# Attention block with a gated expert layer: the last batch of the gating gets a lot of its own

## The chip, the core and the metric

The kernel runs on one core of one Trainium2 chip. The metric is the device time of one execution in microseconds; of the kernel before there are three runs. The core has five engines that run their own instruction streams and wait for each other through semaphores: TensorE (PE; PEld is its weight load), VectorE (DVE), ScalarE (ACT), GpSimd (POOL) and SyncE (SP), which here only issues DMAs. POOL issues the indirect DMAs (rows scattered or gathered by an index per partition).

## The reference

```python
x = x + attention(layernorm(x))           # x: [8, 512, 128], 16 heads of 8, causal, learned relative keys and values
h = layernorm(x)                          # 4096 tokens
scores = softmax(h @ gate_w.T)            # 8 experts
idx = top_k(scores + gate_bias, 2)
weights = scores[idx]
y = sum over e of gate_e * ((silu(h @ w1[e].T) * (h @ w3[e].T)) @ w2[e].T)      # gate_e: the weight, 0 if e is not chosen
z = (silu(h @ sw1.T) * (h @ sw3.T)) @ sw2.T                                      # two shared experts, 256 hidden
out = x + y + z
```

## The kernel before, in words

**Attention.** Two batch elements (32 heads) are worked together: four groups, each with four row tiles of 128 rows, in the order 2, 0, 1, 3 (`ROWS`). So there are 16 rows of work, called rows 0 to 15 here (in the code `e`); a row yields two tiles of 128 tokens. A row tile has eight quads of four heads; row tile 0 takes four heads in a unit (they are narrow), row tile 1 two, row tiles 2 and 3 one. The units, 352, are the slots `m` of one software pipeline. In a slot VectorE copies a turned probability tile (L1156) and takes the minima of the scores (L1171), ScalarE takes the exponentials (L1091), TensorE multiplies and turns (L920, L932, L949, L965), POOL masks the near probabilities (L867, L871, L875). SP moves the relative scores through HBM (`put_rel`, `get_near`), some slots ahead.

**Gating beside attention.** When a row is projected (`pj`), VectorE adds the residual and takes the moments (L1209, L1609, L1612), POOL normalises it (`normalise`, L1555 to L1570), TensorE turns it and takes the eight scores. Four rows, one group, are a batch. For a batch VectorE does a chain of 25 small steps (`chain_op`, L1677 to L1725), two to a slot: softmax, two maxima, weights, and, after a rank product of TensorE (`ranks`), the place of every token in its expert's region of the HBM tensor `slots`. `chain_slots` sets the slots. POOL then scatters the batch's 8 tiles twice, once for each chosen expert (`spread`, L1583, 16 indirect DMAs).

**Expert part.** Two lots: groups 0 to 2 (lot A) and group 3 (lot B). For a lot VectorE computes a map (`map_op`, 14 steps, L1744 to L1776): which expert and which region a block of 128 slots has. Two blocks are a pair; there are 28 pairs in lot A and 12 in lot B. The shared experts are cut into 24 items (for each of 8 chunks of 512 tokens two hidden products, L1851 and L1853, and one sum, L1862). `expert_steps` writes all 64 items into one list of steps that every engine follows: 8 shared items, the pairs of lot A with 12 shared items between them, the pairs of lot B with one, then 3 shared items. A pair takes five steps: turn (L1810), hidden products one step later (L1819), turn of the hidden state after three (L1827), product after four (L1834), and VectorE's weighing (`weigh`, L1927). POOL then scatters the pair's two blocks into the HBM tensor `parts` (`put_parts`, L1591, two indirect DMAs). SP loads a pair's two tiles six steps ahead (`load_pair`, L1457, L1461), in order, once the results of the pair `NX` = 9 earlier have landed; `weigh` reuses one of `NY` = 4 result buffers when a scatter has landed.

The attention of the last row (row 15) is finished inside the first expert steps (`last_row`), and so is the gating of group 3: turn at step 9, scores at 10, chain in steps 11 to 17, map at 18, spreads from step 18 on, one a step. At the end SP loads for each chunk the two parts of its tokens (`load_rest`, L1479 and L1480), VectorE adds them (`finish`, L1946, L1949), SP stores (L1484). Chunks 6 and 7 belong to lot B and come last.

Of the kernel before, what the change touches and what calls it, by code (L numbers as in the profile page):

```python
# [14 lines left out]
P = 128  # L15
# [28 lines left out]
LOTS = [G - 1, 1]  # L44
CAPS = [n * GB * T + P for n in LOTS]
LOT_AT = [0, E * CAPS[0] + P]
SLOTS_ALL = LOT_AT[1] + E * CAPS[1] + P
PAIRS = [(TOPK * n * GB * NI + E) // 2 for n in LOTS]
NPAIR = sum(PAIRS)
NX = 9  # L50
NY = 4
# [56 lines left out]
EARLY = NI * (G - 1)  # L108
CHAIN = 25
MAP = 14  # L110
MAP_PAD = 2

# [87 lines left out]
RIDE_RK = {NI * g + NI + 1: g for g in range(G - 1)}  # L200
# [3 lines left out]
def norm_quads():  # L204

    return {e: max(q for q in range(NQ) if last(q) + 4 <= SLOT_OF["pj", e] + 3) for e in range(GI - 1)}
# [5 lines left out]
def chain_slots():  # L212

    at = {}
    for g in range(G - 1):
        scored, ranked = SLOT_OF["pj", NI * g + NI] + 1, SLOT_OF["pj", NI * g + NI + 1] + 1
        for k in range(CHAIN):
            if k != 20:
                at.setdefault(scored + 1 + k // 2 + (1 if k >= 2 else 0) if k < 20 else ranked + 1 + (k - 21) // 2, []).append((g, k))
    return at  # L220
# [3 lines left out]
EXP_AT = {SLOT_OF["pj", NI * g + NI] + 3: g for g in range(G - 1)}  # L224


def spread_quads():

    at = {}
    for g in range(G - 1):  # L230
        ready = SLOT_OF["pj", NI * g + NI + 1] + 3
        free = [q for q in range(NQ) if last(q) + 4 >= ready and row(q) >= 2 and q not in NORM_AT.values()
                and (row(q) == NI - 1 or q % QUADS < QUADS - 2)]
        left = list(range(TOPK * GB * NI))
        for q in free:
            if left:
                at[q] = (g, left[0], 2)
                left = left[2:]
# [4 lines left out]
SPREAD_LEFT = max(first + many for g, first, many in SPREAD_AT.values() if g == G - 2)  # L243
# [368 lines left out]
def attention_part(nc, t, x, w_attn, w_proj, e_k, e_k127, e_k127h, e_v, e_v127, part_of_row, qk_rows, v_dram, w_slots,  # L612
                   x1_dram, experts_of):
    with ExitStack() as ctx:
# [31 lines left out]
        t["x1"] = x1  # L646
        nmin = sb("nmin", [P, MINS], F32)
# [71 lines left out]
        with nc.Block() as block:  # L719

            @block.sync
            def _(sp):
# [91 lines left out]
                for m in range(SLOTS):  # L814
# [43 lines left out]
            def _(pool):  # L858
# [21 lines left out]
                for q in range(NQ):  # L880
# [3 lines left out]
                    if q == (NI + 1) * QUADS:  # L884
# [261 lines left out]
            def _(dve):  # L1146
# [84 lines left out]
                def last_row(step):  # L1231

                    if step == TURN_STEP + 1:
                        experts["copy_scores"](dve, GI - 1, misc("lg", GI - 1))
                    for k in CHAIN_STEPS.get(step, ()):
                        experts["chain"](dve, G - 1, k, misc("rk", G - 1) if k == 20 else None)
                    for lot in range(2):
                        if step == MAP_STEP[lot]:
                            for k in range(MAP):
                                experts["map"](dve, lot, k)  # L1240
# [4 lines left out]
                    if step == 6:  # L1245
                        residual(GI - 1)

# [4 lines left out]
EARLY_STEPS = 8  # L1252
A_SHARED = 12
# [48 lines left out]
FINISH_AT = {LAST_A + 9 + c: c for c in range(GB * LOTS[0])}  # L1302
REST_AT = {LAST_A + (5 + c if c < 2 else 8 + c): c for c in range(GB * LOTS[0])}
STORE_AT = {step + 1: c for step, c in FINISH_AT.items()}


def expert_part(nc, ctx, t, ps, x1_done, ynT_done, lgr_done, chain, pj_ready, exp_done, x1_dram, xT_dram, slots, parts, gate_w, gate_bias, w123, out):
# [8 lines left out]
    rows_a = sb("rows_a", [P, GB * NI * TOPK * ROWW], F32)  # L1316
    turned = t["both"][:, :, GB * P:2 * GB * P]
    few = sb("few", [P, 3 * GB * NI * E + E + 2 * E + 7 * GB * NI + 2 * GB * NI + 3 * E + 3 * GB], F32)
    upper = sb("upper", [P, P], BF16)
    ones = sb("ones", [P, P], BF16)  # L1320
    chosen = sb("chosen", [P, (GB * NI + 1) * E], BF16)
    place = sb("place", [P, 2, TOPK * GB * NI], I32)
    N8 = GB * NI
    lgr_v, lg_v, score_v, base, caps_v, red_v, sum_v, gw, gb, order, half, var, yy = carve(
# [716 lines left out]
```

## Time and profile before

| | us |
|---|---|
| median of 3 runs (755.0 to 764.2) | 759.09 |
| the profiled execution | 755.63 |
| its span, first to last instruction | 753.8 |
| PE busy | 625.8 (83%) |
| DVE busy | 537.3 (71%) |
| ACT busy | 475.1 (63%) |
| POOL busy | 467.2 (62%) |
| mean granted clock of PE | 0.959 |

The span has a part that loads and projects (to about 50 us), the attention pipeline (to about 557 us) and the expert part. A share over the whole span mixes them; the stretches below are cut by row tile, and by lot in the expert part. In a timeline the bracket behind a row is the engine's idle time ahead of it and what ended it; a row with a count (x10) merges neighbouring instructions of one line. For POOL's indirect DMAs the time is that of making the descriptors; when the data has landed is seen in the chain of waits and at the waiting engine.

### The profile page before, as it was taken

The page shows a single profiled execution, that of the slowest core. Times are in us where ns is not written, and L with a number is a line of the kernel's source. Part 1 is how long each engine was busy: PE and PEld are TensorE (multiplying, and loading weights), DVE is VectorE, ACT ScalarE, POOL GpSimd, SP SyncE. Part 2 cuts the span into 40 slices and gives each one's busy share as a digit, 9 for nine tenths or more (in the row PEclk, how much of TensorE's full clock was granted, in tenths as well). Part 3 has the DMA queues.
Part 4 walks back from the last instruction along what each step waited for, and adds up shares of the span by engine and source line. Part 5 has one row for each costly group of instructions (what it writes and reads, how often), then busy time and mean ns, then how long its engine had stood idle before and what let it go on. Part 6 is the DMA issues. An engine that isn't in the chain of part 4 may idle for free. (4 is left out here: it accounts for less than half of the span.)

```text
span 753.8 us, 27462 instructions
## 1 busy us (share of the span) xinstructions
PE 625.8 (83%) x10116; PEld 473.7 (63%) x10116; DVE 537.3 (71%) x1840; ACT 475.1 (63%) x987; POOL 467.2 (62%) x536
## 2 busy tenths in 40 slices
PE   4667978998898999898989989899968778878671
PEld 2455657687676767676767767677754556666551
DVE  7866677888588899778879878879944365334382
ACT  2686877788688878788876888887751233213210
POOL 9443455665456658778555887756684256777662
PEclk9988989999999999999999999999997999989997
DMA  9899998779978777888767977986623334334582
GB/s 251 254 279 329 325 313 260 238 224 278 311 234 263 234 234 211 255 249 248 240 210 224 256 224 232 277 240 193 238 77 95 103 91 116 116 90 113 144 237 86
DMA packets 150227, 161.89 MB, mean 215 GB/s; under 512 B 13676, under 2 KB 115825, under 8 KB 149776
## 3 DMA queue, kind: packets, MB, share of 16 engines
q1 hardware_dynamic: 145488, 151.67, 67.6%
q0 software_dynamic: 4608, 8.47, 3.3%
q8 instruction: 82, 1.34, 0.7%
q14 instruction: 49, 0.40, 0.2%
HBM read 93.87 MB, written 67.26 MB: 214 GB/s over the span
## 5 line engine op out<-in xcount | busy, mean ns | idle before, releaser
L1171 DVE CUSTOM_DVE_ANT_0 ps<-ps,near 128x128 f32<-128x128 f32 (+3 forms) x512 | 244.5, 508 | 78.7 <-PE ps L920 59.0
L1091 ACT ACTIVATE work<-ps,nmin 128x128 f32<-128x128 f32 (+3 forms) x512 | 248.6, 547 | 68.6 <-DVE nmin L1171 59.6
L932 PE MATMUL ps<-ident,work 128*128 128x128 f32 x1280 | 204.0, 278 | 20.2 <-issue 15.2
L932 PEld LDWEIGHTS ps<-ident,work 128*128 128x128 f32 x1280 | 156.6, 143 | 46.2 <-issue 23.6
L871 POOL TENSOR_SCALAR_AFFINE_SELECT work<-work 128x512 f32<-128x512 f32 x96 | 61.6, 642 | 137.6 <-ACT work L1080 111.4
L920 PE MATMUL ps<-kb,qb 128*128 128x128 bf16 (+3 forms) x512 | 131.3, 308 | 13.6 <-ACT work L1091 9.4
L1156 DVE COPY work<-ps 128x512 f32<-128x512 f32 (+1 forms) x192 | 123.2, 642 | 13.2 <-POOL work L875 8.1
L875 POOL TENSOR_TENSOR work<-work 128x512 f32<-128x512 f32 x96 | 124.2, 1294 | 8.0
L1591 POOL DMA_INDIRECT parts<-near x80 | 79.1, 989 | 46.6 <-DVE near L1927 25.5
L1080 ACT ACTIVATE work<-ps 128x512 f32<-128x512 f32 (+1 forms) x160 | 90.0, 562 | 18.3 <-PE ps L932 16.6
L949 PE MATMUL ps<-work,vb 128*9 128x128 f32 x2560 | 96.5, 277 | 5.8 <-ACT relS L1067 2.2
L1067 ACT ACTIVATE relS<-ps 128x512 f32<-128x512 f32 x128 | 84.3, 660 | 12.7 <-PE ps L907 11.4
L949 PEld LDWEIGHTS ps<-work,vb 128*9 128x9 f32 x2560 | 57.7, 90 | 28.8 <-issue 21.9
L1171 DVE DVE_READ_ACCUMULATOR2_ANT nmin<- 128x1 f32 x512 | 72.0, 141 | 0.0
L965 PE MATMUL ps<-tv,work 128*32 128x8 f32 x4096 | 58.8, 180 | 12.8 <-POOL work L875 7.0
L965 PEld LDWEIGHTS ps<-tv,work 128*32 128x32 f32 x4096 | 48.3, 114 | 32.6 <-issue 25.2
L920 PEld LDWEIGHTS ps<-kb,qb 128*128 128x128 bf16 x512 | 40.7, 98 | 33.6 <-ACT work L1091 15.6
L907 PE MATMUL ps<-te,qb 128*128 128x128 bf16 x512 | 51.2, 224 | 7.4 <-ACT relS L1067 5.5
L1894 ACT ACTIVATE near<-ps 128x256 f32<-128x256 f32 x40 | 15.4, 384 | 58.1 <-PE ps L1819 58.1
L907 PEld LDWEIGHTS ps<-te,qb 128*128 128x128 bf16 x512 | 35.0, 99 | 22.6 <-issue 14.8
L1819 PE MATMUL ps<-qb,near 128*128 x160 | 45.7, 411 | 1.3 <-ACT near L1889 0.7
L867 POOL COPY work<-work 128x512 f32<-128x512 f32 x32 | 34.7, 1094 | 15.7 <-DVE work L1156 15.7
(172 smaller groups left out, 835.6 us busy)
## 6 DMA issues: line engine op xcount, KB each, us to landing
near<-w_slots SPq DMA_DIRECT2D x96, 512.0 KB, 5.2
w_slots<-relS SPq DMA_DIRECT2D x128, 256.0 KB, 4.6
qk_rows<-work SPq DMA_DIRECT2D x36, 256.0 KB, 4.7
near<-w_slots SPq DMA_DIRECT2D x32, 256.0 KB, 4.5
near<-slots SPq DMA_DIRECT2D x80, 65.0 KB, 1.9
qb<-parts SPq DMA_DIRECT2D x16, 256.0 KB, 3.7
qk_rows<-y SPq DMA_DIRECT2D x9, 256.0 KB, 6.7
qb<-qk_rows SPq DMA_DIRECT2D x24, 96.0 KB
```

The lines of the kernel that those rows point to most:

```text
L875: nc.gpsimd.tensor_tensor(dst, ptmp[:, :, :], pT[:, q % 2, :, i * P:(i + 1) * P], ALU.add).then_inc(pc_done, 1)
L907: ins = nc.tensor.matmul(bank[:, h * P:(h + 1) * P], qb[:, 4 * u + h, i * P:(i + 1) * P], te[:, :], start=True, stop=True)
L920: ins = nc.tensor.matmul(qk_ps[:, m % 3, h * wide:(h + 1) * wide], qb[:, n, i * P:(i + 1) * P], kb[:, n // 4 * 2 + n % 2, 0:wide], start=T ...
L932: ins = nc.tensor.transpose(tp_ps[:, m % 2, n * P:(n + 1) * P], prob[:, m % PROBS, n * P:(n + 1) * P], ident[:, :])
L949: ins = nc.tensor.matmul(bank[32 * h:32 * h + VD, a * P:(a + 1) * P], vb[:, g % 2, b * NI + j, n * VD:(n + 1) * VD], pT[:, q % 2, h, j * P ...
L965: ins = nc.tensor.matmul(bank[32 * tq:32 * tq + NH, a * D:(a + 1) * D], pcT[:, e % 2, tau, :], tv[:, tau, :], start=True, stop=True)
L1067: nc.scalar.activation(relS[:, q % RSLOTS, :, :, :].rearrange("p a j h -> p a h j"), misc("rel", q).rearrange("p (a h j) -> p a h j", a=2, ...
L1080: nc.scalar.activation(pT[:, q % 2, n * w:n * (w + 1), 0:wide], tp_ps[:, m % 2, 0:n * wide].rearrange("p (h s) -> p h s", h=n), ACT.Copy). ...
L1091: ins = nc.scalar.activation(prob[:, m % PROBS, h * wide:(h + 1) * wide], qk_ps[:, m % 3, h * wide:(h + 1) * wide], ACT.Exp, bias=nmin[:, ...
L1156: nc.vector.tensor_copy(pT[:, q % 2, n * w:n * (w + 1), 0:wide], tp_ps[:, m % 2, 0:n * wide].rearrange("p (h s) -> p h s", h=n)).then_inc( ...
L1171: nc.vector.tensor_tensor_reduce(out=scores, in0=scores, in1=near[:, q % NEAR, a, 4 * P - wide:4 * P, r], scale=1.0, scalar=3e38, op0=ALU. ...
L1591: nc.gpsimd.indirect_dma_start(out=parts, out_offset=bass.IndirectOffsetOnAxis(ap=tiles[j % NX][:, u, META:META + 1].bitcast(I32), axis=0) ...
```

## The change

The batches become 3, 4, 4 and 5 rows: rows 0 to 2, 3 to 6, 7 to 10 are lot A (44 tiles scattered, 26 pairs), rows 11 to 15 are lot B (20 tiles, 14 pairs). Every chain starts one row earlier than the group's end did.

Lot B has an HBM tensor of its own, `slots_b`: the experts' blocks lie packed, with no empty space between regions, so a pair's tiles have fixed addresses and SP reads no register for them. Since the unused slots of such a block are not known ahead, SP clears `slots_b` and the ends of lot A's regions whole, once, in the attention (`clear_blocks`). A short map of 8 steps (`late_map_op`) works on all partitions inside chain 3. Lot B's results are not scattered: VectorE writes them to a buffer of their own, SP stores each pair whole to `ys` (`put_sums`), and when all 14 are stored POOL gathers, for each of the last 10 tiles, the two rows of every token by the places that the spread used (`fetch_sums`, 20 indirect DMAs). Lot A's parts are loaded and added as before, by chunk; chunks 4 and 5 have three tiles from lot A and one from lot B.

In the list of steps 5 shared items come first, 6 ride in lot A, 1 in lot B, and 12 come behind the last pair. Lot A's map is at step 0 instead of 2, the spreads of lot B come two a step from step 18, `NX` is 8 and `NY` 6.

```diff
-LOTS = [G - 1, 1]
+BATCHES = [range(0, 3), range(3, 7), range(7, 11), range(11, 16)]
+BATCHES_OF = [range(0, 3), range(3, 4)]
...
-NX = 9
-NY = 4
+NX = 8
+NY = 6
...
 def chain_slots():
-    for g in range(G - 1):
-        scored, ranked = SLOT_OF["pj", NI * g + NI] + 1, SLOT_OF["pj", NI * g + NI + 1] + 1
+    for m, rows in enumerate(BATCHES[:-1]):
+        scored, ranked = SLOT_OF["pj", rows.stop] + 1, SLOT_OF["pj", rows.stop + 1] + 1
...
+                    if m == SLOT_OF["pj", 5]:
+                        experts["clear"](sp)
...
-EARLY_STEPS = 8
-A_SHARED = 12
+EARLY_STEPS = 5
+A_SHARED = 6
...
-MAP_STEP = (2, 18)
-SPREAD_STEPS = {18 + k: k for k in range(TOPK * GB * NI)}
+MAP_STEP = 0
+SPREAD_STEPS = {18 + k: k for k in range(TILES_OF[-1])}
...
+    def clear_blocks(sp):
+        sp.wait_ge(table_done, 4)
+        sp.dma_start(slots_b.rearrange("(k p) c -> p k c", p=P),
+                     pad_row.unsqueeze(1).broadcast_to([P, 2 * PAIRS[1], ROWW])).then_inc(pad_out, 16)
+        at = E * CAPS[0]
+        sp.dma_start(slots[at:at + E * P, :].rearrange("(k p) c -> p k c", p=P),
+                     pad_row.unsqueeze(1).broadcast_to([P, E, ROWW])).then_inc(pad_out, 16)
...
     def load_pair(sp, j):
...
-        if j >= NX:
+        if j >= NX + PAIRS[0]:
+            sp.wait_ge(y_done, j - NX + 1)
+        elif j >= NX:
             sp.wait_ge(part_out[j % NX], part_count(j - NX))
+        if j >= PAIRS[0]:
+            for u in range(2):
+                at = (2 * (j - PAIRS[0]) + u) * P
+                sp.dma_start(tiles[j % NX][:, u, :], slots_b[at:at + P, :]).then_inc(tile_in[j % NX], 16)
+            return
...
+    def put_sums(sp, j):
+        sp.wait_ge(y_done, j + 1)
+        at = 2 * (j - PAIRS[0]) * P
+        sp.dma_start(ys[at:at + 2 * P, :].rearrange("(u p) c -> p u c", p=P), late_y[:, j - PAIRS[0], :, :]).then_inc(late_out, 16)
...
         for step in range(STEPS):
-            if step == 7:
+            if step == FIRST_PAIR:
+                keep_turned(sp, GI - 2)
                 store(GI - 1)
...
+            for at, j in PAIR_AT.items():
+                if step == at + 5 and j >= PAIRS[0]:
+                    put_sums(sp, j)
             if step in REST_AT:
                 load_rest(sp, REST_AT[step])
...
+    def fetch_sums(pool):
+        m = len(BATCHES) - 1
+        pool.wait_ge(late_out, 16 * PAIRS[1])
+        for n, (tile, at) in enumerate(FETCH):
+            for k in range(TOPK):
+                source = place[:, m % 2, k * TILES_OF[m] + tile:k * TILES_OF[m] + tile + 1]
+                nc.gpsimd.indirect_dma_start(out=gath[:, k, at, :], out_offset=None, in_=ys,
+                                             in_offset=bass.IndirectOffsetOnAxis(ap=source, axis=0),
+                                             bounds_check=2 * PAIRS[1] * P - 1, oob_is_err=False
+                                             ).then_inc(gath_in[n >= FETCH_FIRST], 16)
...
     def pool_program(pool):
-        for n in range(SPREAD_LEFT, TOPK * N8):
-            spread(pool, G - 2, n, 1)
+        normalise(pool, GI - 2)
+        for n in range(SPREAD_LEFT, TOPK * TILES_OF[-2]):
+            spread(pool, len(BATCHES) - 2, n, 1)
         normalise(pool, GI - 1)
         for step in range(STEPS):
-            if step - 4 in PAIR_AT:
+            if step - 4 in PAIR_AT and PAIR_AT[step - 4] < PAIRS[0]:
                 put_parts(pool, PAIR_AT[step - 4])
             if step in SPREAD_STEPS:
-                spread(pool, G - 1, SPREAD_STEPS[step], 1)
+                spread(pool, len(BATCHES) - 1, 2 * SPREAD_STEPS[step], 2)
+        fetch_sums(pool)
```

POOL's program behind the last normalisation, before (`parts<-near` is a scatter of results, `slots<-work,place` a spread; 35072, 8192 and 3584 are rows of the HBM tensors):

```order
L1570 TENSOR_SCALAR work<-work,mv,rstd 128x2x128 x2
L1591 DMA parts<-near 8192x128 x10
L1583 DMA slots<-work,place 35072x130
L1591 DMA parts<-near 8192x128 x2
...
L1583 DMA slots<-work,place 35072x130
L1591 DMA parts<-near 8192x128 x48
```

and now:

```order
L1629 TENSOR_SCALAR work<-work,mv,rstd 128x2x128 x2
L1662 DMA parts<-near 8192x128 x18
L1642 DMA slots_b<-work,place 3584x130 x4
...
L1642 DMA slots_b<-work,place 3584x130 x2
L1662 DMA parts<-near 8192x128 x20
L1653 DMA work<-ys,place 128x128 x20
```

Of the scatters 52 are left, the last 20 stand behind the last spread, and the gathers (`work<-ys,place`) close the program.

VectorE in row tile 0 of the second group, before: minima (`ISA ps,nmin`), four to a slot, and copies (L1156):

```order
L1171 ISA nmin 128x1
L1156 COPY work<-ps 128x384
L1171 ISA ps,nmin<-ps,near 128x128
L1171 ISA nmin 128x1
L1171 ISA ps,nmin<-ps,near 128x128
```

and now, with two steps of the chain (here 2 and 3, `few<-few`) behind each slot's four minima:

```order
L1178 ISA ps,nmin<-ps,near 128x128
L1178 ISA nmin 128x1
L1762 TENSOR_REDUCE few<-few 128x6
L1764 RECIPROCAL few<-few 128x6
L1163 COPY work<-ps 128x384
L1178 ISA ps,nmin<-ps,near 128x128
```

Seven such pairs of steps stand in the eight slots of this row tile, in each of the three batches; before they stood in row tile 3.

SP while lot B runs, now (`near<-slots_b` are tiles of a pair, `qb<-parts` the two parts of a chunk, `ys<-work` a pair's results, `out<-kb` a chunk of the result):

```order
L1529 DMA qb<-parts 128x4x128
L1504 DMA near<-slots_b 128x130 x2
L1542 DMA ys<-work 128x2x128
L1504 DMA near<-slots_b 128x130 x2
L1542 DMA ys<-work 128x2x128
L1504 DMA near<-slots_b 128x130 x2
L1542 DMA ys<-work 128x2x128 x2
L1528 DMA qb<-parts 128x4x128
L1529 DMA qb<-parts 128x4x128
L1537 DMA out<-kb 128x4x128
```

The first row is the load for chunk 1, the tiles are those of pairs 37, 38 and 39, and the load for chunk 2 stands behind them and behind the results of pairs 26 to 29.

## Rows read from the trace of the kernel before

**Rows 1.** Stretches (--windows): us, busy time of PE, PEld, DVE, ACT, POOL; clock, DMA share, GB/s.

```profile
136.00:182.00 46.00, 42.95 (x853) 33.91 (x844) 38.38 (x113) 35.42 (x62) 26.16 (x37) 1.00 0.79 233
347.00:359.00 12.00, 10.49 (x228) 7.76 (x227) 10.97 (x65) 11.16 (x38) 10.13 (x14) 1.00 0.90 270
388.00:434.00 46.00, 43.48 (x856) 33.43 (x851) 42.44 (x137) 34.71 (x61) 31.75 (x42) 1.00 0.79 228
676.00:714.00 38.00, 31.49 (x183) 24.49 (x181) 16.28 (x40) 11.84 (x30) 28.85 (x31) 1.00 0.44 122
```

**Rows 2.** Timeline of POOL: start, duration, line, operation [idle before, its releaser].

```profile
605.06 1.11 POOL L1591 DMA_INDIRECT parts<-near  x1 [9.57 <-DVE near L1927]
703.17 0.97 POOL L1591 DMA_INDIRECT parts<-near  x1 [0.30 <-issue]
740.73 0.97 POOL L1591 DMA_INDIRECT parts<-near  x1 [0.30 <-issue]
```

**Rows 3.** Chain of waits, lot A and last chunk: start, duration, what.

```profile
675.04 2.42 DMA parts<-near
677.48 0.59 SPq L1457
678.76 2.10 DMA near<-slots
745.10 4.13 DMA qb<-parts
```

**Rows 4.** Timeline of five engines between attention and the first pair.

```profile
556.66 0.24 POOL L1555 TENSOR_SCALAR few<-mv 128x2 f32<-128x2 f32 x1
...
563.46 1.90 PE L965 MATMUL ps<-tv,work 128*32 128x8 f32 x128 [4.01 <-POOL work L875]
...
573.63 0.15 DVE L1744 TENSOR_TENSOR work<-few 1x8 f32<-1x8 f32 x1
...
576.21 1.02 PE L1853 MATMUL ps<-vb,qb 128*128 128x512 f32 x2
...
590.79 0.23 POOL L1555 TENSOR_SCALAR few<-mv 128x2 f32<-128x2 f32 x1 [11.38 <-DVE mv L1612]
...
591.71 7.02 SPq L1461 DMA_DIRECT2D near<-slots  x10
...
594.21 0.41 PE L1810 MATMUL ps<-ident,near 128*128 128x128 f32 x2 [1.95 <-DMA near<-slots]
```

**Rows 5.** Timeline of DVE: a ranking chain's two operations, and a row tile of 128 columns.

```profile
265.59 0.21 DVE L1677 TENSOR_REDUCE few<-few 128x8 f32<-128x64 f32 x1
265.84 0.22 DVE L1679 TENSOR_TENSOR few<-few 128x64 f32<-128x64 f32 x1
...
353.08 0.69 DVE L1156 COPY work<-ps 128x512 f32<-128x512 f32 x1 [1.03 <-POOL work L875]
```

**Rows 6.** Timeline of PE and DVE while lot B runs.

```profile
698.29 0.44 PE L1810 MATMUL ps<-ident,near 128*128 128x128 f32 x2 [0.32 <-DMA near<-slots]
711.51 0.38 PE L1810 MATMUL ps<-ident,near 128*128 128x128 f32 x2
...
715.13 0.69 DVE L1946 TENSOR_TENSOR kb<-kb,qb 128x512 f32<-128x512 f32 x1 [5.95 <-DMA qb<-parts]
...
717.03 0.66 PE L1827 MATMUL ps<-ident,near 128*128 128x128 f32 x2 [5.14 <-DVE near L1915]
717.49 1.91 PE L1819 MATMUL ps<-qb,near 128*128 x4
```

**Rows 7.** Timeline of POOL and DVE, then DMA issues (count, KB each, us to landing).

```profile
725.01 1.43 POOL L1591 DMA_INDIRECT parts<-near  x1 [1.08 <-DVE near L1927]
...
750.05 0.69 DVE L1949 TENSOR_TENSOR qb<-kb,qb 128x512 f32<-128x512 f32 x1
...
x_dram<-work SPq DMA_DIRECT2D x16, 128.0 KB, 3.1
qb<-in_w SPq DMA_DIRECT2D x1, 1920.0 KB, 8.6
```

More of the change, by code:

```diff
@@ L43 @@
 META = C
-LOTS = [G - 1, 1]
[L45 to L48, printed above, removed]
+BATCHES = [range(0, 3), range(3, 7), range(7, 11), range(11, 16)]
+BATCHES_OF = [range(0, 3), range(3, 4)]
+BATCH_OF = {e: m for m, rows in enumerate(BATCHES) for e in rows}
+LOT_OF = [lot for lot, batches in enumerate(BATCHES_OF) for m in batches]
+TILES_OF = [GB * len(rows) for rows in BATCHES]
+LOT_TILES = [sum(TILES_OF[m] for m in batches) for batches in BATCHES_OF]
+CAPS = [n * P + P for n in LOT_TILES]
+SLOTS_ALL = E * (CAPS[0] + P)
+PAIRS = [(TOPK * n + E) // 2 for n in LOT_TILES]
 NPAIR = sum(PAIRS)
-NX = 9
-NY = 4
+NX = 8
+NY = 6
 SCRATCH = 2048
@@ L1298, with finish_steps, fetch_order, expert_part @@
 RANK_STEP = 16
-MAP_STEP = (2, 18)
-SPREAD_STEPS = {18 + k: k for k in range(TOPK * GB * NI)}
+MAP_STEP = 0
+SPREAD_STEPS = {18 + k: k for k in range(TILES_OF[-1])}
 LAST_A = max(step for step, j in PAIR_AT.items() if j < PAIRS[0])
[L1302 to L1307, printed above, removed]
+FIRST_TILES = [sum(BATCH_OF[e] in BATCHES_OF[0] for e in range(NI * (c // GB), NI * (c // GB + 1))) for c in range(CHUNKS)]
+WITH_PARTS = sum(n > 0 for n in FIRST_TILES)
+def finish_steps():
+    at, step = {}, LAST_A + 8
+    for c in range(WITH_PARTS):
+        step = max(step, *[s for s, item in SHARED_AT.items() if item == ("product", c)]) + 1
+        at[step] = c
+    return at
+FINISH_AT = finish_steps()
+REST_AT = {LAST_A + 5: 0, LAST_A + 6: 1, **{step + 1: c + 2 for step, c in FINISH_AT.items() if c + 2 < WITH_PARTS}}
+STORE_AT = {step + 1: c for step, c in FINISH_AT.items() if FIRST_TILES[c] == CH // P}
+def fetch_order():
+    order = []
+    for c in range(CHUNKS):
+        g, b = divmod(c, GB)
+        for i in range(FIRST_TILES[c], NI):
+            order.append((GB * (NI * g + ROWS.index(i) - BATCHES[-1].start) + b, len(order)))
+    return order
+FETCH = fetch_order()
+FETCH_FIRST = sum(CH // P - n for n in FIRST_TILES[0:CHUNKS - 1])
+def expert_part(nc, ctx, t, ps, x1_done, ynT_done, lgr_done, chain, pj_ready, exp_done, x1_dram, xT_dram, slots, slots_b, parts, ys, gate_w, gate_bias, w123, out):
     CT = CH // P
@@ L1655, in ranks, with exponentials @@
-    def ranks(pe, g, bank):
-        if g == 0:
-            pe.wait_ge(const_done, 2)
-        pe.wait_ge(chain, CHAIN * g + 18)
-        wide = (N8 + 1) * E
-        nc.tensor.matmul(bank[:, 0:wide], upper[:, :], chosen[:, :], start=True, stop=False, skip_group_check=True)
-        for n in range(N8):
+        wait(dve, chain, CHAIN * (m - 1) + 2)
+        nc.vector.tensor_copy(lgr_v[:, at * E:(at + GB) * E], bank[:, 0:GB * E]).then_inc(lgr_done, 1)
+    def exponentials(act, m):
+        act.wait_ge(chain, CHAIN * m + 2)
+        wide = TILES_OF[m] * E
+        nc.scalar.activation(score_v[:, 0:wide], lg_v[:, 0:wide], ACT.Exp).then_inc(ex_done, 1)
```

352 lines of the change are left out of this document (202 added, 150 removed).

## The prediction

> **What bounds the kernel now.** I read the table of stretches first. In the attention part (to about 557 us) TensorE is busy 93 to 95% of a stretch of row tile 3; in row tile 0 no single engine leads: VectorE is busy 10.97 of 12 us, ScalarE 11.16, TensorE 10.49 [rows 1]. In the expert part TensorE is still busy 31 of 38 us at the full clock, but the timeline of POOL names what holds it: the 72 indirect transfers that belong to lot A (56 scatters of results, 16 spreads of the last batch) start between 605.06 and 703.17 us, and 24 scatters of lot B follow, up to 740.73 [rows 2]. In a run without a wait one takes 0.97 us and 0.30 us pass before the next, so 1.277 us each; 72 of them are 91.9 us, and only 6 us of the 98 are gaps. The chain of waits shows how this reaches the others: a scatter lands 2.42 us after its start, SP then reads a register for 0.59 us, issues the tile that reuses the buffer, and TensorE gets it 2.10 us later [rows 3].
>
> So I divide the time at T, the landing of lot A's last scatter: before, 703.17 + 2.42 = 705.6 us, and 48.2 us follow to the end of the span, 753.8.
>
> **Attention: the ranking chain moves.** The batch of 3 rows shifts every chain by one row tile: its steps 0 to 19 sat in row tile 3 and now sit at the end of row tile 2, in row tile 0 and at the start of row tile 1, in all three batches. 14 of them fall into the seven slots of row tile 0, two a slot. One follows the other after 0.25 us [rows 5], so 3.5 us of VectorE per batch. Row tile 0 takes 12 us and VectorE has 1.03 us idle there, waiting for POOL [rows 1, 5]; ScalarE is as full, but a later minimum delays its exponentials one for one. Row tile 3 gives little back: with a chain VectorE is busy 42.4 us, without one 38.4, and the stretch is 46 us in both cases, since TensorE has 43 us [rows 1]. Cost per batch between 0 (all hidden) and 3.7 us (nothing hidden, and a short wait for the exponentials); I take 1.7, because the buffers ahead of row tile 0 differ: **+5 us** for three, ends 0 and 11.
>
> **Attention: the cleared blocks.** SP gets two stores more, 2.4 MB in all, in row tile 3 of the second pair. A load of 1.9 MB landed in 8.6 us [rows 7]; DMA is 79% busy there [rows 1]. The near loads behind them on SP's queue are issued some nine slots, 13 us, ahead, and land in about 5. I take 0; without that cover it would be 8.
>
> The extra iota of each normalisation is POOL time beside TensorE's 95%; I cost it at nothing, hidden by that slack (31.75 of 46 us busy [rows 1]).
>
> **The front of the expert part.** Times on the old scale, without the attention term.
> - POOL ran the normalisation of row 14 (556.66 to 561.33) ahead of the last masks, and the last value products waited for them until 563.46 [rows 4]. Now two spreads (2 x 1.277) stand there instead of 4.7 us: they start at 561.3, 2.1 us earlier.
> - Lot A's map (14 steps on VectorE, 573.63 to 578.9) moves into the idle time before 569; pads and the last spreads are then done by about 573.
> - SP no longer waits for row 15's residual before the first tile. It waits for the fourth shared product, 576.21 + 1.0 - 2.1 = 575.1, reads registers, and issues at 576.8 what it issued at 591.71; TensorE turns tile 0 some 2.5 us later, at 579.3, as against 594.21 [rows 4].
> - The first scatter comes later than 10.9 us after that, since TensorE's product 0 now stands behind the turn of row 15, which waits for POOL's normalisation. That one moves from 590.79 to about 585.4 (residual behind pair 0's multiplication) and takes 4.8; with turn, product, weighing and wake-up the first scatter starts at 591.9 instead of 605.06. Ends: 599.7 if it gains only POOL's 5.4, 590.2 if the full 14.9; I take 591.9, the value of the chain in program order.
> - Lot A has 52 scatters and 20 spreads, again 72. Gaps: after 9 pairs' scatters POOL waits for the pairs of the steps in which the chain and two table loads run, about 3 us; and with 8 buffers instead of 9 the loop over four pairs (landing 2.42, register and load 3.4, products 1.9, weighing 0.5, two scatters 2.55) is 2.7 us a pair against 2.55, about 1.4 us over the last ten. Last start 591.9 + 71 x 1.277 + 4.4 = 687.0, so **T = 689.4, 16.2 us earlier**. The bound without gaps is 684.9.
>
> **Behind T.** Here the change pays.
> - Tile 33 waits for the last scatter of lot A; without a register read it reaches TensorE after 2.7 us. Seven pairs follow at 2.2 us each (six took 13.2 us from 698.29 to 711.51 [rows 6]): 15.4. The last pair's remaining steps have two hidden products and one sum of the shared experts between them, since only 6 instead of 12 shared items ride in lot A: 3 x 1.95 + 3.3 + 0.4 = 9.6 us. Together 27.7.
> - VectorE adds chunks 0 to 2 in these steps and waits in order for their parts. Before, the same wait was 5.95 us, stopped TensorE for 5.14, and the next products ran cold, 1.91 us instead of 1.03 [rows 6]. Now the load for chunk 2 stands on SP behind the load of pair 39, which waits for pair 31's weighing: issued at T + 16, landed 4 us later, while VectorE is ready 6.5 us before that. TensorE then lacks two hidden states: 7.5 us, 2 for chunk 0, 1.5 for the lower clock: 11. Lowest 0.
> - The last result store: 0.4 to issue and 2.4 (128 KB took 3.1 from issue to landing [rows 7]): 2.8.
> - 20 gathers. No row shows one; the nearest is the scatter of 128 rows, 1.277, with bounds 0.97 and 1.43 [rows 2, 7]. 19 x 1.277, a wake-up and 2.4 to land: 26.8. No other work of POOL covers them, and the remaining 10 shared items (about 20 us) end inside them.
> - One scatter that ran beside VectorE's sums of two SBUF operands took 1.43 instead of 0.97 us [rows 7]; four such sums fall into the gathers, about 0.6 us for the halves that meet. The Trainium skill (SBUF — State Buffer, section Who interferes with whom) has it that such a sum contends only with GpSimd instructions that read SBUF and infers that descriptor generation needs the write interface; by that this term would be 0, and the trace does not agree.
> - Two sums of 0.7, then store: 750.05 + 0.69 to 753.8 is 3.1 us [rows 7]: 4.5.
>
> Sum behind T: 27.7 + 11 + 2.8 + 26.8 + 0.6 + 4.5 = 73.4, against 48.2: **+25.2**.
>
> **Sum.** -16.2 + 25.2 + 5 = **+14 us** on the profiled execution, 755.63, so 769.6. The median of the runs, 759.09, lies 3.5 above that one; prediction **773 us**, +1.8%. About 1% is what a measurement of this kernel can tell from no change.
>
> **Rivals.**
> 1. No change, because VectorE's queue does not bite: if chunk 2's parts land before VectorE asks, the 11 us fall away, and the sum is +3: 762 us. For it: the loads of 256 KB land in about 4 us [rows 3], and before only the first add waited long. Against: SP's order. It decides if VectorE's idle time before chunk 2's first add is under 2 us. Chance 0.17.
> 2. No change, because gathers are cheaper than scatters: at 0.8 us each 9.5 us go, +4.5: 763 us. For it: the words that follow the scatters land in HBM, these in SBUF. Against: descriptors are made in the same number. Chance 0.08.
> 3. Not slower, or faster: the front gains all (T = 684.9), nothing stalls behind T (62.4) and row tile 0 hides the chain. Span 747, 752 us by the median, below 751 with cheaper gathers too. Against: three favourable things at once. Chance 0.14, most of it around 752 to 757.
> 4. Slower still: row tile 0 hides nothing (+6) or POOL starves in lot A, because with 8 buffers the pairs wait for each other and the shared work is gone as filler (+5): 779 to 784. TensorE has 6.5 us free in 38 [rows 1], which speaks against the second. Chance 0.12.
>
> The forecast itself, 766 to 779, has 0.49. Range 752 to 785: 0.09 lies below, about as much above. Faster by over 1%: 0.11 (the good part of 3, and what I overlooked); within 1%: 0.27 (1, 2, the rest of 3); slower by over 1%: 0.62.
>
> **What would show it.** In the changed kernel's timeline: row tile 0 of the second to fourth pair at 14 us instead of 12; the first scatter near 592 plus the attention term; 72 transfers from there in about 95 us; an idle time of VectorE of 5 to 8 us before chunk 2's add with TensorE idle behind it; POOL idle for some 40 us, then 20 gathers at 1.28 us as the last thing but one add and one store. I am wrong if the gathers start less than 30 us behind T, or if row tile 0 keeps its 12 us.

## The result and the profile after

The changed kernel took 784.9 us (median of 4 runs, 779.4 to 788.5), the kernel before 757.05 beside it (4 runs, 751.2 to 764.2): a ratio of **1.039** (95% interval 1.034 to 1.045), 28 us slower. The forecast was slower by 14 us, 1.8%. The direction was right, the size half of what came. The ratios below leave out runs more than 1.5% above the fastest of their kernel, which matters once, in the last experiment: three of its six runs are left out, and the median of all six is 747.7 us, 2.0% below the kernel before.

The profiled execution took 788.47 us, span 786.8, 33 us more than the 753.8 of before. Its own median is 3.6 us lower, so this pair of traces shows some 5 us more than the medians do. Four marks cut both spans: the start of the last exponential of the attention, the start of the first scatter of results, the start of the last transfer of lot A, and the end.

| us | before | after | difference | forecast |
|---|---|---|---|---|
| to the last exponential of the attention | 555.8 | 571.8 | +16.0 | +5 |
| from there to the first scatter | 49.3 | 38.0 | -11.3 | -13.2 |
| lot A's 72 transfers, first start to last | 98.1 | 99.1 | +1.0 | -3.0 |
| from that start to the end of the span | 50.6 | 78.0 | +27.3 | +25.2 |
| span | 753.8 | 786.8 | +33.0 | +14.0 |

POOL's timeline of the changed kernel has the marks (start, duration, operation, idle time ahead and what ended it); the first two rows answer to the first two of [rows 2], the other three have no row before:

```profile
609.75 1.10 POOL L1662 DMA_INDIRECT parts<-near  x1 [2.27 <-DVE near L2039]
708.84 0.97 POOL L1662 DMA_INDIRECT parts<-near  x1 [0.30 <-issue]
754.80 1.06 POOL L1653 DMA_INDIRECT work<-ys,place  x1 [44.99 <-DMA ys<-work]
774.42 1.22 POOL L1653 DMA_INDIRECT work<-ys,place  x1 [0.30 <-issue]
779.85 0.99 POOL L1653 DMA_INDIRECT work<-ys,place  x1 [0.30 <-issue]
```

POOL idles for 45 us while lot B is computed, and then 20 gathers close the program, the tail that was forecast. The large miss is the attention. The time from the first exponential of a row tile to that of the next, in the order of work, says where (each row tile has 32 exponentials; the last one of the fourth group ends at its last exponential's end):

| us, second to fourth group | row tile 2 | row tile 0 | row tile 1 | row tile 3 |
|---|---|---|---|---|
| before | 41.1, 38.4, 38.0 | 13.19, 12.70, 12.67 | 25.3, 27.4, 25.3 | 47.4, 46.8, 46.4 |
| after | 42.2, 37.9, 40.5 | **14.82, 16.22, 16.23** | 24.9, 27.1, 26.0 | **53.7**, 45.4, 45.2 |

Row tile 0 lost 8.7 us in three groups, row tile 3 of the second group 6.3; row tile 3 of the other two gave 2.6 back. Row tile 2 lost 3.1, but there single traces differ by as much: with the attention of before, its third and fourth times are 38.4 and 38.0 here, 40.9 and 40.1 in another kernel below. The expectations below quote row tile 0 as 15.8, 17.3 and 17.3; those values count from the last exponential of the row tile ahead, one too early.

**Row tile 0.** Stretches of the third group's row tile 0, before and after, and of its row tile 3 after (columns as in [rows 1]):

```profile
347.28:359.98 12.70, 10.69 (x227) 7.72 (x224) 11.67 (x67) 11.86 (x40) 10.60 (x15) 1.00 0.88 267
355.90:372.12 16.22, 11.83 (x221) 7.97 (x219) 15.49 (x81) 12.38 (x41) 10.16 (x12) 0.89 0.79 237
398.00:444.00 46.00, 44.23 (x870) 35.01 (x872) 39.99 (x118) 35.96 (x63) 36.27 (x47) 1.00 0.79 230
```

VectorE was busy 11.67 of 12.70 us; now, with 14 instructions more, it is busy 15.49 of 16.22, and ScalarE, TensorE and POOL are not. Of the 3.8 us that were added 0.3 are covered. Pieces of VectorE's timeline (step 1 of the chain, at 353.20, still belongs to row tile 2, step 2, at 357.29, waits for the chain's own exponential on ScalarE):

```profile
353.20 1.13 DVE L1759 TENSOR_TENSOR few<-few 128x64 f32<-128x64 f32 x1
...
357.29 0.22 DVE L1762 TENSOR_REDUCE few<-few 128x8 f32<-128x64 f32 x1 [0.49 <-ACT few L1728]
...
359.07 0.73 DVE L1766 TENSOR_TENSOR few<-few 128x64 f32<-128x64 f32 x1
359.84 1.32 DVE L1772 TENSOR_TENSOR work<-few 128x64 f32<-128x64 f32 x1
...
364.41 0.68 DVE L1163 COPY work<-ps 128x512 f32<-128x512 f32 x1
...
366.39 0.68 DVE L1163 COPY work<-ps 128x512 f32<-128x512 f32 x1
```

and POOL's beside the first:

```profile
359.09 0.63 POOL L878 TENSOR_SCALAR_AFFINE_SELECT work<-work 128x512 f32<-128x512 f32 x1
359.81 1.28 POOL L882 TENSOR_TENSOR work<-work 128x512 f32<-128x512 f32 x1
```

From copy to copy a slot takes 1.98 us; before, it took 1.55 in the last slots of this row tile (four minima and a copy), with no idle time:

```profile
354.64 0.69 DVE L1156 COPY work<-ps 128x512 f32<-128x512 f32 x1
...
356.19 0.69 DVE L1156 COPY work<-ps 128x512 f32<-128x512 f32 x1
```

So two steps of the chain lengthen a slot by 0.43 of their 0.50 us. On top, the chain's products at 359.07 and 359.84 take 0.73 and 1.32 us instead of 0.24 (as they do in the last chain, on wider rows) and end when POOL's operation ends (359.72 and 361.09). The Trainium skill (SBUF — State Buffer, section Who interferes with whom) says that a VectorE instruction with two SBUF inputs contends with a GpSimd instruction that reads SBUF; these rows agree, 1.32 against 0.24 us. In row tile 3 before, one step of each chain met POOL as well (1.33 us each time), but there TensorE was busy 43 of 46 us.

**The cleared blocks.** SP's timeline 20 us into the second group's row tile 3 (264.23 to 317.96):

```profile
284.20 0.38 SPq L1475 DMA_DIRECT2D slots_b<-work  x1
284.62 6.93 SPq L1478 DMA_DIRECT2D slots<-work  x1
291.60 2.70 SPq L1471 DMA_DIRECT2D xT_dram<-both  x1
294.39 1.55 SPq L771 DMA_DIRECT2D near<-w_slots  x1
```

and VectorE's:

```profile
302.59 0.70 DVE L1178 CUSTOM_DVE_ANT_0 ps<-ps,near 128x512 f32<-128x512 f32 x1 [5.51 <-DMA near<-w_slots]
```

The second clearing store, 0.5 MB behind one of 1.9 MB, occupies SP for 6.93 us, and the small store behind it for 2.70. The load of near scores that stands next is issued at 294.39, and VectorE waits 5.51 us for it. In five traces with both stores in this place (this one and four below) the row tile took 53.7 to 55.4 us, in four without the large store 45.3 to 47.5.

**Behind lot A.** VectorE's adds (kb is the chunk; the first row answers to the add of [rows 6]):

```profile
720.19 1.42 DVE L2061 TENSOR_TENSOR kb<-kb,qb 128x512 f32<-128x512 f32 x2 [2.78 <-DMA qb<-parts]
...
731.61 1.42 DVE L2061 TENSOR_TENSOR kb<-kb,qb 128x512 f32<-128x512 f32 x2 [5.94 <-issue]
...
782.56 1.42 DVE L2061 TENSOR_TENSOR kb<-kb,work 128x512 f32<-128x512 f32 x2 [7.79 <-DMA work<-ys,place]
```

and TensorE behind the second of them:

```profile
733.50 0.66 PE L1938 MATMUL ps<-ident,near 128*128 128x128 f32 x2 [6.28 <-DVE near L2026]
733.96 1.91 PE L1930 MATMUL ps<-qb,near 128*128 x4
```

```profile
733.50:736.00 2.50, 2.50 (x8) 2.14 (x9) 0.94 (x3) 0.09 (x1) 0.00 (x0) 0.50 1.15 342
```

This is the forecast stall: VectorE waits 5.94 us for chunk 2 (the row names no releaser, but where the load is issued earlier, below, the wait is 2 us), TensorE lacks its hidden states for 6.28, and its next products take 1.91 us instead of 1.03, at a granted clock of 0.50 (the last row), the lower of its two levels, 1.2 GHz.

### The profile page after: what moved, and what is told of

Its sections match the earlier page's. It is cut to its first block and busy times, and to the rows that moved or that the text cites. A ratio compares the mean times of both kernels' runs of the same rounds, so it can differ in the third digit from the quotient of the medians.

```text
span 786.8 us, 27347 instructions
## 1 busy us (share of the span) xinstructions
PE 635.0 (81%) x10116; PEld 485.1 (62%) x10116; DVE 545.7 (69%) x1834; ACT 475.0 (60%) x987; POOL 461.1 (59%) x539
## 5 line engine op out<-in xcount | busy, mean ns | idle before, releaser
L939 PE MATMUL ps<-ident,work 128*128 128x128 f32 x1280 | 206.8, 282 | 25.8 <-issue 20.5
L939 PEld LDWEIGHTS ps<-ident,work 128*128 128x128 f32 x1280 | 159.5, 145 | 51.3 <-issue 28.9
L927 PE MATMUL ps<-kb,qb 128*128 128x128 bf16 (+3 forms) x512 | 132.2, 310 | 13.7 <-ACT work L1098 10.9
L972 PEld LDWEIGHTS ps<-tv,work 128*32 128x32 f32 x4096 | 47.7, 112 | 33.5 <-issue 27.3
L1662 POOL DMA_INDIRECT parts<-near x52 | 50.8, 977 | 26.0 <-DVE near L2039 13.2
L1930 PE MATMUL ps<-qb,near 128*128 x160 | 53.0, 464 | 0.0
L2031 DVE TENSOR_TENSOR near<-near,ps 128x256 f32<-128x256 f32 x40 | 16.8, 420 | 48.7 <-ACT near L2005 45.3
```

Source lines behind the costliest of these rows:

```text
L927: ins = nc.tensor.matmul(qk_ps[:, m % 3, h * wide:(h + 1) * wide], qb[:, n, i * P:(i + 1) * P], kb[:, n // 4 * 2 + n % 2, 0:wide], start=T ...
L939: ins = nc.tensor.transpose(tp_ps[:, m % 2, n * P:(n + 1) * P], prob[:, m % PROBS, n * P:(n + 1) * P], ident[:, :])
L972: ins = nc.tensor.matmul(bank[32 * tq:32 * tq + NH, a * D:(a + 1) * D], pcT[:, e % 2, tau, :], tv[:, tau, :], start=True, stop=True)
```

## The experiments

Each kernel ran beside the kernel before on its chip; four chips were used, so two ratios differ only where their intervals do. Code cuts are marked with three dots. Row tiles are given as in the table above.

**The chain out of row tile 0.**

```diff
-... scored + 1 + k // 2 + (1 if k >= 2 else 0) if k < 20 ...
+... scored + 1 + k // 2 + (14 if k >= 2 else 0) if k < 20 ...
```

> The changed kernel with steps 2 to 19 of every ranking chain 13 slots later: out of row tile 0, into the second half of row tile 1. Theory (VectorE has no free time in row tile 0, so the chain is paid there whole, and more where its operations on two SBUF operands wait for POOL): row tile 0 of the second to fourth group falls from 15.8, 17.3 and 17.3 us to about 13 each, row tile 1 grows by 1 to 3 us each since VectorE is 85% busy there; together 4 to 9 us less than the changed kernel, ratio to before 1.028 to 1.034 instead of 1.039. Rival (the long row tiles come from a lower clock or from DMA, not from the chain): row tile 0 stays at 16 to 17 us, ratio 1.039.

Ratio 1.033 (1.025 to 1.041): within what was expected, but its interval and the change's overlap. Row tile 0 fell to 12.9, 12.2 and 14.3 us, 7.8 less in all, so the chain was what made it long. But row tile 1 grew to 28.0, 30.5 and 29.2, 9.7 more, and the last exponential came at 577.4 instead of 571.8. The theory of the place is confirmed, that the move pays is not shown: the chain was not hidden in row tile 1 either.

**The clearing stores at the end of the attention.**

```diff
...
-if m == SLOT_OF["pj", 5]:
+if m == max(READ_AT) + 1:
     experts["clear"](sp)
```

> The changed kernel with the two clearing stores (2.4 MB) issued behind the last load of near scores of the attention instead of in row tile 3 of the second group. Theory (the stores keep DMA busy while the near scores of the next units are due): row tile 3 of the second group falls from 53.1 us to 46 to 47, nothing else moves, since the stores end before the pads need them; 6 to 7 us less than the changed kernel, ratio to before about 1.031. Rival (that row tile is long for another reason, such as the loads of the next group's queries and keys): 53 us stays, ratio 1.039. Second rival (the stores delay the first expert tiles): the row tile is mended, the first scatter comes as much later, ratio 1.039.

Ratio 1.039 (1.029 to 1.048): nothing won. Row tile 3 of the second group fell to 45.3 us as expected, but that of the fourth rose from 45.2 to 55.8. That is the ratio of the second rival, reached inside the attention; the first scatter came only 2.1 us later. SP and VectorE there:

```profile
544.49 0.66 SPq L1475 DMA_DIRECT2D slots_b<-work  x1
545.20 12.22 SPq L1478 DMA_DIRECT2D slots<-work  x1
557.47 3.33 SPq L780 DMA_DIRECT2D xr<-in_x  x1
```

```profile
568.77 0.17 DVE L1723 COPY few<-ps 128x16 f32<-128x16 f32 x1 [10.41 <-DMA xr<-in_x]
```

All loads of near scores stood ahead this time. What was held was the next load on SP's queue, row 14's residual (`xr<-in_x`), and VectorE, in order, waited 10.41 us for it. What the stores hold is whatever stands next on SP's queue, not the loads of near scores as such.

**Chunk 2's parts earlier, twice.** In the first version the loads for chunks 2 to 5 go two steps ahead, in the second chunk 5's stays.

```diff
-**{step + 1: c + 2 for step, c in FINISH_AT.items() ...}
+**{step - 1: c + 2 for step, c in FINISH_AT.items() ...}              # first
+**{step + (1 if c == 3 else -1): c + 2 for step, c in FINISH_AT.items() ...}   # second
```

> The changed kernel with the loads of the parts of chunks 2 to 5 two steps earlier on SP's queue, so that chunk 2's stands ahead of the tiles of pair 38. Theory (VectorE waits in order for chunk 2, and TensorE behind it): the idle time of 5.94 us before chunk 2's add falls under 1 us, and from the last scatter of lot A to the first gather it takes 37 to 39 us instead of 43.5 (45.0 us idle on POOL now); 5 to 6 us less, ratio to before 1.031 to 1.033. Rival (the pairs are held by SP's queue in another way, by the tiles of pair 38 that now wait behind this load): the wait moves to TensorE's turn of pair 38, under 2 us less.

Ratio 1.0405 (1.032 to 1.050): no gain. The wait before chunk 2's add fell from 5.94 to 2.21 us and the last weighing ended at 742.6, 36.8 us behind the start of lot A's last scatter instead of 41.7. SP then lost it again:

```profile
739.57 0.86 SPq L1542 DMA_DIRECT2D ys<-work  x1
745.85 0.36 SPq L1528 DMA_DIRECT2D qb<-parts  x1
746.26 0.48 SPq L1529 DMA_DIRECT2D qb<-parts  x1
746.86 0.41 SPq L1522 DMA_DIRECT2D qb<-x_dram  x1
747.32 1.02 SPq L1542 DMA_DIRECT2D ys<-work  x2
```

Chunk 5's load now stood ahead of the last two stores of results and waited for its buffer until 745.85; the gathers wait for those stores.

> The changed kernel with the loads of the parts of chunks 2 to 4 two steps earlier on SP's queue, chunk 5's left where it was (in the run before, chunk 5's load held the last two stores of results until its buffer was free, from 742.6 to 747.3 us). Theory (the stall of VectorE on chunk 2 costs the tail 5 us): the last weighing stands 37 us behind the last scatter of lot A instead of 41, and now the first gather follows too, 40 to 41 us behind the last scatter's start instead of 46; 5 us less than the changed kernel, ratio to before about 1.032. Rival (the tail is bound by the stores and the shared products, not by the stall): 45 to 46 us stay, ratio 1.039.

Ratio **1.026** (1.020 to 1.032). The first gather starts 40.0 us behind the last scatter (748.35 and 708.38) instead of 46.0, and the wait before chunk 2's add was 1.95 us: the stall was worth 6 us of the tail, and the rival fell. The ratio shows more than that, 10 us; its interval and the one of the change leave about 5 us of play.

**Batches of four rows, the rest of the change kept.**

```diff
-BATCHES = [range(0, 3), range(3, 7), range(7, 11), range(11, 16)]
+BATCHES = [range(0, 4), range(4, 8), range(8, 12), range(12, 16)]
```

> The changed kernel with batches of 4, 4, 4 and 4 rows: all else of the change stays (packed blocks, stores of whole results, gathers, the early first pair). The chain goes back to row tile 3, lot A has 28 pairs and 16 spreads (72 transfers as before), lot B 12 pairs and 16 gathers. Theory (the batch split costs the chain in row tile 0 and a longer tail): 8 us less in the attention, 2 pairs less behind the last scatter of lot A (4.4 us) and 4 gathers less (5.2 us): 17 to 18 us less than the changed kernel, ratio to before 1.014 to 1.018. Rival (the cost lies in the packed lot and the gathers themselves and in the cleared blocks, not in the split): 5 to 10 us less, 1.026 to 1.033.

Ratio **1.0115** (1.004 to 1.019), 2.7% less than the change: the split into 3, 4, 4 and 5 rows is most of the loss, a little more than was expected, and the rival fell. In its trace, against the changed kernel's: the attention ends 7.4 us earlier (row tile 0 at 13.7, 12.7 and 12.8), the stretch to the first scatter is 4.2 longer, lot A 2.1 shorter, the first gather stands 33.7 us behind the last scatter instead of 46.0, and the gathers take 4.9 less; together 22.4, the whole difference of the spans (764.4 and 786.8). Of the 12.3 in the tail two pairs at 2.2 us each [rows 6] account for 4.4; with two pairs less chunk 2's load no longer stands behind their tiles, and its add waits 1.53 us instead of 5.94, and chunk 0's 1.44 instead of 2.78; some 2 us stay unaccounted for:

```profile
719.88 0.69 DVE L2061 TENSOR_TENSOR kb<-kb,qb 128x512 f32<-128x512 f32 x1 [1.53 <-issue]
```

Against the kernel before, its attention ends 8.6 us later, and 6.7 of them are the second group's row tile 3 (54.1 us), where the clearing stores stayed.

**The packed blocks cleared in the expert part.** Only lot A's 0.5 MB are cleared in the attention; the 1.9 MB follow the first five pairs' tiles on SP's queue.

```diff
             if step == FIRST_PAIR:
+                clear_late(sp)            # the first of the two stores of clear_blocks
...
```

> The changed kernel with the clearing of the packed blocks (1.9 MB) issued behind the first five pairs' tiles in the expert part, and only the 0.5 MB of lot A's regions cleared in the attention. Theory (1.9 MB of stores cost 6 to 8 us wherever loads of near scores are due, nothing where DMA is 30 to 40% busy): row tile 3 of the second group at 46 to 48 us as against 53, row tile 3 of the fourth at 45 to 47, no scatter later; 5 to 7 us less, ratio to before about 1.031. Rival (the stores hold the tiles of pairs 5 to 9): the first ten scatters take 5 us longer, ratio 1.036 to 1.039.

Ratio **1.031** (1.025 to 1.037). Row tile 3 of the second group 46.0 us, of the fourth 45.3, the first scatter 6.2 us earlier. Lot A's transfers then took 102.0 us instead of 99.1: part of the rival came true as well. The 0.5 MB alone cost SP nothing, and the hold moved along with the large store, to the DMA behind it (the first row is from the attention):

```profile
285.25 0.40 SPq L1476 DMA_DIRECT2D slots<-work  x1
...
593.45 0.43 SPq L1480 DMA_DIRECT2D slots_b<-work  x1
593.93 6.24 SPq L1471 DMA_DIRECT2D xT_dram<-both  x1
```

> The changed kernel with batches of 4, 4, 4 and 4 rows and the clearing of the packed blocks (now 1.6 MB) in the expert part, as in the two runs that did each alone. Theory (the two costs add up): 1.0115 less 5 to 7 us is 1.003 to 1.005. Rival (the clearing is hidden in neither place, or holds the first tiles): 1.0115 stays.

The same edit with batches of four: 1.009 (1.006 to 1.013). The first scatter came 4.5 us earlier than with batches of four alone, lot A took 2.5 longer; 2 us were left, less than expected and less than the intervals resolve, so the rival is not excluded.

> The changed kernel with both repairs at once: the loads of the parts of chunks 2 to 4 two steps earlier, and the packed blocks cleared in the expert part; batches stay at 3, 4, 4 and 5 rows. Theory (the stall and the clearing are terms of their own and add): about 1.3% and 0.8% off 1.039, ratio to before 1.017 to 1.021; what is left is the chain in row tile 0, two pairs and four gathers more, which the batches of 4 do not have. Rival (they hide each other, or the chips of the runs differed more than the kernels): 1.025 to 1.031, no better than one of them.

Both repairs at 3, 4, 4 and 5 rows: 1.026 (1.020 to 1.032), which is the rival's number, while its span, 767.1, is 19.7 us below the changed kernel's. That the terms add is not shown. This run also tells what one trace is worth: its attention code is that of the first run of this edit, which ran on another chip, and took 505.8 us from the first to the last exponential as against 512.8 there.

**What an operation costs in row tile 0.** The kernel before with 14 operations, two behind the minima of seven slots, in row tile 0 of the third and fourth group.

```diff
+                    for g in (2, 3):
+                        if m - FIRST[QUADS * (NI * g + 1)] in range(1, 8):
+                            experts["extra"](dve)
+                            experts["extra"](dve)
...
+        nc.vector.tensor_tensor(tmp, biased, score, ALU.add).then_inc(extra_done, 1)             # first
+        nc.vector.tensor_scalar(tmp, score, 1.0, None, ALU.mult).then_inc(extra_done, 1)         # second
...
```

> The kernel before with 14 more VectorE operations, two behind the minima of each of seven slots, in row tile 0 of the third and fourth group alone: the sum of two SBUF operands, 128 x 64, one behind the other, its result never read. Theory (VectorE has nothing free in row tile 0, so each operation is paid whole, and an operation on two SBUF operands also waits for the end of a POOL operation that runs at that moment): those row tiles go from 12.7 and 12.9 us to 16 to 17.5, three or more of the 28 operations take 0.5 us or more instead of 0.22. Rival (about half is hidden in VectorE's idle time, as forecast): 14 to 14.8 us.

> The same with operations that read one SBUF operand (a product with a constant, 128 x 64), 14 to a row tile. Theory: no wait for POOL, all of the 28 take about 0.2 us; the row tiles grow by the 14 operations alone, 2.5 to 3.5 us, to 15 to 16.3 us, so less than with two operands. Rival (half hidden): 14 to 14.8 us as with two operands.

Row tile 0 went from 12.70 and 12.67 us to 15.44 and 15.46 with two operands, to 15.25 and 15.75 with one. The third group's, two operands and then one:

```profile
347.29:362.73 15.44, 11.46 (x227) 7.75 (x224) 15.20 (x80) 12.18 (x41) 10.48 (x14) 1.00 0.86 252
348.17:363.42 15.25, 12.41 (x228) 8.76 (x224) 15.01 (x81) 12.23 (x41) 10.07 (x12) 0.89 0.87 249
```

VectorE's idle time fell from 1.03 us to 0.24; of the 3.5 us that the two-operand kernel added to its busy time 0.8 were covered and 2.7 paid. The rival, half hidden, fell in both, but so did the theory for two operands: its 16 to 17.5 us were not reached, and one operation a row tile, not three in the two, took over 0.5 us. One operand gave the length that was expected. The wait for POOL did not tell them apart: in either kernel one pair a row tile was long, here with two operands and then with one,

```profile
351.27 1.75 DVE L1738 TENSOR_TENSOR work<-work,few 128x64 f32<-128x64 f32 x2
```

```profile
351.91 1.52 DVE L1738 TENSOR_SCALAR work<-few 128x64 f32<-128x64 f32 x2
```

and it ended with POOL's masking product in both (351.67 + 1.28, and 352.10 + 1.28). The same section of the Trainium skill (SBUF — State Buffer, Who interferes with whom) lists tensor_scalar among the operations that can take the port shared with GpSimd, under conditions on its operands; the 1.52 us agrees, and the expectation that one operand is free of it was wrong.

**The front of the change on the kernel before.**

```diff
-EARLY_STEPS = 8
-A_SHARED = 12
+EARLY_STEPS = 5
+A_SHARED = 15
...
-MAP_STEP = (2, 18)
+MAP_STEP = (0, 18)
...
-            if step == 3:
+            if step == 1:
                 store_pads(sp, 0)
-            if step == 6:
+            if step == FIRST_PAIR:
                 keep_turned(sp, EARLY + 2)
-            if step == 7:
                 store(GI - 1)
...
     def pool_program(pool):
+        normalise(pool, GI - 2)
```

> The kernel before with the front of the change alone: five shared items ahead of the first pair instead of eight (the three others ride in lot A behind its tenth pair), lot A's map at step 0, its pads at step 1, the store of row 15's residual behind the first pairs' tiles, row 14's normalisation behind the last masks. Batches, scatters of lot B and the end are those of before. Theory (the front of the change gained 11 us from the end of attention to the first scatter, and the rest of it lost 40): the first scatter 9 to 12 us earlier than 605.1, lot A's 72 transfers take the 98 us of before to at most 4 more, the end is that of before; 6 to 11 us less than before, ratio 0.985 to 0.992. Rival (the gain is lost in lot A, since the pairs then wait for each other and POOL idles): the last scatter of lot A no earlier, ratio 0.998 to 1.003.

Ratio **0.986** (0.981 to 0.992): faster than before, by a little over 1%, as expected. The first scatter starts at 599.6, 5.5 us earlier, not 9 to 12; the stretch to it is 42.3 us (49.3 before, 38.0 in the change), and lot A takes 96.1 instead of 98.1, where at least 98 was expected.

> The faster front on the kernel before, and VectorE's adds of chunks 0 to 5 two steps later in its order (the loads of their parts as they were, the stores with the adds). Theory (VectorE waits in order for chunk 0's parts, 4.4 us, and POOL then lacks results for 2.9 and 1.8 us): these gaps of POOL fall to under 1 us, the last scatter comes 3 to 5 us earlier, ratio to before 0.979 to 0.983 instead of 0.986. Rival (the wait only moves to the end, where the last chunks are added behind the last scatter): the same 0.986.

```diff
-FINISH_AT = {LAST_A + 9 + c: c for c in range(GB * LOTS[0])}
-REST_AT = {LAST_A + (5 + c if c < 2 else 8 + c): c for c in range(GB * LOTS[0])}
+FINISH_AT = {LAST_A + 11 + c: c for c in range(GB * LOTS[0])}
+REST_AT = {LAST_A + (5 + c if c < 2 else 10 + c): c for c in range(GB * LOTS[0])}
```

The loads of the parts of chunks 2 to 5 moved with the adds, then, and only those of chunks 0 and 1 stayed as they were.

Ratio **0.975** (0.967 to 0.983), the lowest of all; that it beats the run above (0.986) is not shown, since the intervals overlap. VectorE's wait for chunk 0, 4.42 us in the run above, is gone, and the last scatter starts at 729.74 instead of 732.58; 1.4 us of that were gained ahead of the first scatter, which the edit does not touch. POOL's gaps became shorter but not under 1 us, which the theory expected. In the run above, then in this:

```profile
710.78 1.07 POOL L1591 DMA_INDIRECT parts<-near  x1 [2.94 <-DVE near L1928]
717.65 1.26 POOL L1591 DMA_INDIRECT parts<-near  x1 [1.75 <-DVE near L1928]
```

```profile
713.41 1.25 POOL L1591 DMA_INDIRECT parts<-near  x1 [2.29 <-DVE near L1928]
725.53 1.35 POOL L1591 DMA_INDIRECT parts<-near  x1 [1.47 <-DVE near L1928]
```

## Why the prediction was right in kind and half in size

The step that failed is the attention: +5 us taken, +16.0 measured, 11 of the 19 us by which the pair of traces missed the forecast. Two of its terms were wrong.

- **The cleared blocks (0 taken, 8 without cover).** The cover named was nine slots between the issue of a near load and its use. It assumed that SP goes on issuing while the stores run; SP stood for 6.93 + 2.70 us instead, and the load behind was issued that much later. Measured 6.3 in that row tile, 7.6 beside the 1.3 that each of the other two row tiles 3 gained: the price without cover. The runs with the large store elsewhere show it.
- **Row tile 0 (+5 taken, ends 0 and 11).** 8.7 measured, 1.6 in the second group and 3.5 and 3.6 in the next two, where 1.7 each were taken. The text took half as hidden in VectorE's one idle microsecond of a row tile. That idle time stood in one slot and the other slots were full; 0.3 us of it served as cover, since the chain waits 0.49 for its own exponential, and 0.8 in the kernel with 28 added operations. Steps that met POOL took up to 1.32 us; such a step was in the trace of before, in row tile 3 (1.33), and was not counted.
- **What row tile 3 gave back.** 1.2 to 1.4 us a group, where little was expected. The 46 us "in both cases" of the text are the lengths of the windows that it read; by the exponentials row tile 3 took 45.7 us without a chain (first group) and 46.4 to 47.4 with one.
- **The iota (0 taken).** In the kernel with batches of four, which keeps it, the second to fourth group outside the clearing's row tile took 328.2 us against 327.3 before: nothing that a trace can tell.
- **The front (-13.2 by this mark).** -11.3. The turn of tile 0, expected at 579.3 plus the attention's delay, came at 594.90, that is 578.9 plus 16.0; the first scatter at 609.75, 593.75 plus 16.0, against 591.9.
- **Lot A (-3.0).** +1.0. All gaps of POOL lie in the first 18 transfers, 8.2 us of them, where 4.4 were expected: VectorE works through the chain and the new map from 620 to 635 us, weighings stand behind their steps, and 6.7 of the 8.2 fall there. The last 54 transfers run without a gap, so 8 buffers instead of 9 cost nothing there.
- **Behind T (73.4).** T, the last landing, is seen on SP, which waits for it and issues the next tile at 712.38:

```profile
712.38 2.69 SPq L1504 DMA_DIRECT2D near<-slots_b  x6
```

So 74.4 us follow, and this part of the forecast was right in its parts too: TensorE lacks hidden states for 3.48 and 6.28 us (2 and 7.5 expected); the last weighing ends 38.1 us behind T (38.7 expected); 20 gathers from 754.80, the last landing at 782.4 (27.6 with the landing, 26.8 expected). Three gathers ran beside VectorE's sums and took 1.00, 0.99 and 1.22 us, so the contention was 0.2 and not 0.6. By the inference in the Trainium skill (SBUF — State Buffer, section Who interferes with whom) that descriptor generation needs the write interface, it would be 0, nearer to what was measured than the estimate.
- **The rivals.** Rival 1, where VectorE's queue does not bite, needs the tiles of pairs 38 and 39 out of the way: true with batches of four (1.53 us), not here. Rival 4's time, 779 to 784, came near 784.9 partly by luck: its first half, row tile 0 hides nothing (11 us in all), lies further up than the 8.7 measured, its second half (+5 in lot A) came as 4.0 us, from VectorE's queue and not from the 8 buffers, and the clearing, which it does not name, did the rest.

What stays open: 5 us between the pair of traces and the medians, whether the repairs add, and what the chain costs net. Two traces of one attention code differed by 7 us, as much as the 7.4 us that batches of four gain in the attention.

## What to carry to other kernels

Before chained small operations are moved into a stretch, read the engine's idle time slot by slot: an idle microsecond in one slot covered 0.3 to 0.8 us of the 3.5 to 3.8 that were added to eight slots. A large store can cost its queue too: ask what is issued behind it, and count the time for which the issuing engine stands. Where an in-order engine adds the results of an earlier stage, its wait is set by the order of the load queue, and moving one load ahead can hold the next one, so the whole queue up to the last consumer has to be read again.

## What the hardware showed beside this

The DMA issued right behind the 1.9 MB store held SP for 6.93 us in one place and 12.22 in another, where that DMA was a store of 0.5 MB, and for 6.24 in the expert part, where it was a small store (4.86 behind 1.6 MB); away from it the store of 0.5 MB was issued in 0.40. A gather of 128 rows from HBM took 1.00 us on POOL and 0.30 passed before the next, about 2% more than a scatter's 0.97 and 0.30. VectorE's small operations with two operands mostly stayed at 0.21 to 0.26 us beside POOL's copies (0.22 to 0.24 away from them), while one a batch took 0.49 to 0.51; the longest, 0.73 and 1.32, stood beside the masking select and the product of two operands.
